# Cross-attention experts and a quantised mixture of experts in one kernel: a new order of the first blocks

## The reference

```python
def xattn(h, token_ids, W):                 # W = ctx_2048, [4, 512, 512], used three times
    expert_ids = minimum(clip(token_ids, 0, 24999) // 6250, 3)
    for e in range(4):
        g = silu(h @ W[e].T);  u = h @ W[e].T
        y = (g * u) @ W[e].T                # ctx used as the down matrix too
        out = where(expert_ids == e, y, out)

def ffn(x, router_w, wg, wu, wd):           # 8 experts, ternary weights, int8 activations
    idx = argmax(x @ router_w.T)
    for e in range(8):
        g = bitlinear(x, wg[e]); u = bitlinear(x, wu[e])
        y = bitlinear(relu(g)**2 * u, wd[e])
        out += where(idx == e, y, 0)
# bitlinear: weights round(w / mean|w|) clipped to -1..1, activations round(x * 127 / max|x|)

x = x + xattn(layernorm(x), token_ids, ctx)     # x: [2048, 512] f32
x = x + ffn(layernorm(x), router_w, wg, wu, wd)
```

## Time and profile before

| | us |
|---|---|
| median of 3 runs | 268.15 (267.83 to 268.71) |
| the profiled execution | 267.64 |
| its span in the profile | 265.9 |
| PE, DVE, ACT, POOL busy | 236.1, 214.0, 212.8, 159.6 |

### The profile page before, as it was taken

The page is one execution under the profiler, slowest core; times in us unless marked ns, Lnnn a source line. Parts: engine busy times, 40 slices in busy tenths (PEclk is TensorE's granted clock), DMA queues, the critical chain, the costliest instruction groups (busy, mean ns, idle before and its releaser), DMA issues.

```text
span 265.9 us, 5805 instructions
## 1 busy us (share of the span) xinstructions
PE 236.1 (89%) x1413; PEld 173.5 (65%) x1423; DVE 214.0 (81%) x678; ACT 212.8 (80%) x324; POOL 159.6 (60%) x315
## 2 busy tenths in 40 slices
PE   2285868999999999999999999989969999999980
PEld 2133747888888888888888888877435555555530
DVE  5947898888887787878887887778869899989971
ACT  1886777698898788898888798886779999999960
POOL 4435014477778777767776766257826477556553
PEclk9997999999999999999999999999999999999996
DMA  5997339466654555684556653353257798311110
GB/s 210 429 409 284 137 158 355 159 235 212 220 202 126 198 210 222 255 296 153 211 208 223 210 207 108 160 161 106 110 182 259 251 301 290 119 41 65 60 41 0
DMA packets 13839, 51.72 MB, mean 195 GB/s; under 512 B 2862, under 2 KB 2862, under 8 KB 10224
## 3 DMA queue, kind: packets, MB, share of 16 engines
q1 hardware_dynamic: 8928, 37.91, 39.3%
q0 software_dynamic: 4880, 13.44, 14.3%
HBM read 40.49 MB, written 13.48 MB: 203 GB/s over the span
## 4 chain that ended last, share of the span: by engine, by line
PE 72%; DVE 10%; issue 6%; POOL 5%; DMA 4%; ACT 1%; SPq 0%; POOLq 0%; DVEq 0%
PE bank L1296 35%; PE bank L1397 17%; PE bank L1289 9%; PE bank L1369 5%; PE bank L1391 3%; DVE ctx_lo L828 2%; DMA x<-x_rows,gather 2%; DMA x_rows<-row,store_at 1%; POOL out_rows L529 1%; DMA late_rows<-x_rows 1%; POOL x L434 1%; DVE ternary L796 1%; DVE ternary L851 1%; PE bank L1315 1%; DVE stats L884 1%
## 5 line engine op out<-in xcount | busy, mean ns | idle before, releaser
L1397 PE MATMUL bank<-ternary,qT 128*128 x179 | 43.4, 379 | 0.4
L566 ACT ACTIVATE ternary<-staged 128x2048 bf16<-128x2048 f32 x22 | 42.0, 1910 | 1.2 <-DMA staged<-weight_chunks 1.2
L572 ACT ACTIVATE ternary<-staged,w_scale 128x1536 int16<-128x1536 f32 x22 | 34.5, 1566 | 3.3 <-DVE w_scale L840 3.3
L485 POOL DMA_INDIRECT x_rows<-row,store_at x19 | 25.0, 1314 | 15.6 <-DVE var_eps L892 8.5
L1397 PEld LDWEIGHTS bank<-ternary,qT 128*128 128x128 bf16 x184 | 17.7, 97 | 20.7 <-issue 4.6
L529 POOL DMA_INDIRECT out_rows<-late_rows x18 | 19.8, 1102 | 16.0 <-DVE late_rows L1140 14.3
L434 POOL DMA_INDIRECT x<-x_rows,gather x19 | 21.2, 1114 | 11.5 <-DVE row L934 6.0
L444 POOL TENSOR_TENSOR rstd<-var_eps,half_powers 128x1 f32<-128x1 f32 x19 | 12.5, 657 | 20.7 <-DVE var_eps L892 20.2
L600 ACT ACTIVATE pT_hi<-bank 128x512 fp32r<-128x512 f32 x19 | 11.3, 596 | 15.7 <-PE bank L1289 15.6
L1397 PE MATMUL bank<-ternary,rT 128*128 x87 | 22.6, 379 | 1.0 <-ACT rT L664 0.8
L1296 PE MATMUL bank<-ctx_hi,hT_hi 128*128 x76 | 22.5, 417 | 0.0
(11 more groups left out here) (213 smaller groups left out, 655.8 us busy)
## 6 DMA issues: line engine op xcount, KB each, us to landing
staged<-weight_chunks SPq DMA_DIRECT2D x22, 1024.0 KB, 5.5
late_rows<-x_rows SPq DMA_DIRECT2D x18, 260.0 KB, 3.3
ternary<-ctx_chunks SPq DMA_DIRECT2D x4, 1024.0 KB, 10.9
x_rows<-filler SPq DMA_DIRECT2D x9, 260.0 KB, 5.8
ternary<-weight_chunks SPq DMA_DIRECT2D x2, 1024.0 KB, 5.5
staged<-x_rows SPq DMA_DIRECT2D x5, 260.0 KB, 2.8
x<-x_rows,gather POOLq DMA_INDIRECT x19, 3.5
x_rows<-row,store_at POOLq DMA_INDIRECT x19, 3.4
```

What stands on the lines that cost most here:

```text
L485: pool.indirect_dma_start(x1_rows, bass.IndirectOffsetOnAxis(ap=store_at[b % ROWS][:, :], axis=0), row[b % ROWS][:, :], None, bounds_check ...
L566: nc.scalar.activation(ternary[:, m * K * D:(m + 1) * K * D], staged[i % 2][:, :], ACT.Abs, accum_out=abs_sum[:, 2 * i:2 * i + 1]).then_in ...
L572: nc.scalar.activation(ternary[:, m * K * D + DVE_COLS:(m + 1) * K * D].bitcast(I16), staged[i % 2][:, DVE_COLS:], ACT.Copy, scale=w_scale ...
L1397: last = pe.matmul(ps[:, :], left[:, k * P:(k + 1) * P], ternary[:, bass.ds(e * (3 * K * D) + (kind * K + k) * D, D)], start=(k == 0), sto ...
```

## The change

- **Sorting.** `place_block` is stored as an integer, which rounds it, so the instruction with `MAGIC` (L787) goes. The product of `block_hot` with `token1` goes from DVE to GpSimd, between its first and second tile; GpSimd has three tiles and DVE thirteen. PE takes GpSimd's tiles together before its last. `gather1` is made by one instruction (with 0 instead of -1 where there is no token) before the experts' table.
- **Loads.** SP waits for the fence behind the second gather, and then issues weights 2, context 2, weights 3, context 3. Weights 2 and 3 go into places of their own (matrices 8 to 11 of `ternary`), and weights 4 and 5 take the buffers of 0 and 1.
- **GpSimd** issues four gathers in its prologue with the first power between the third and fourth, and then makes the high halves of the contexts 2 and 3, which ACT did.
- **Layernorm.** h is only x minus its mean; the factor rstd is applied in silu's scale and in the gate (`scalar_tensor_tensor` instead of `tensor_tensor`). So `normalise` waits for the mean alone, and silu waits for rstd. GpSimd's `inverse_deviation(b)` waits for the gate of block b - 2 instead of its h.
- **DVE.** Low halves are made in two instructions of 1024 columns, set between the statistics; those of context 3 stand at the end of tick 2. `variance` is split into `aggregate` and `variance`. The cuts of the matrices 0 to 3 go to the end of the ticks 5 to 8. In tick 2 mean and scale of matrix 4 stand behind `largest`.
- **PE.** `first_product(0)` waits in three steps; products 1 to 3 wait for the low half of their own block's expert, product 4 for all. `WARM_UP` is 4, 5, 4. `sum_mean(0)` stands before the first block's expert is read; `transpose_h(2)` before `sum_mean(3)`; in tick 2 `sum_mean(4)` behind `first_product(2)`.
- **ACT.** In tick 2 `scale_part(4)` stands behind `evict_hT(3)`.

```diff
-WARM_UP = (4, 8, 4)
+WARM_UP = (4, 5, 4)
...
-        place_block = sb("place_block", [P, TILES], F32)
+        place_block = sb("place_block", [P, TILES], I32)
...
+        staged_early = [spare(8, 2 * K * D, F32), spare(10, 2 * K * D, F32)]
+        def staged_of(i):
+            return staged_early[i - 2] if i in (2, 3) else staged[i % 2][:, :]
...
-        POOL_TILES = TILES * 2 // 7
+        POOL_TILES = 3
...
             def load_weights(i):
-                if i >= 2:
-                    sp.wait_ge(dve_part, i - 1)
-                    sp.wait_ge(act_part, i - 1)
-                sp.dma_start(staged[i % 2][:, :], weights_in[ORDER[i]]).then_inc(staged_in[i % 2], 16)
+                if i in (2, 3):
+                    sp.dma_start(staged_of(i), weights_in[ORDER[i]]).then_inc(staged_early_in[i - 2], 16)
+                    return
+                if i >= 4:
+                    last = i - 4 if i < 6 else i - 2
+                    sp.wait_ge(dve_part, last + 1)
+                    sp.wait_ge(act_part, last + 1)
+                sp.dma_start(staged_of(i), weights_in[ORDER[i]]).then_inc(staged_in[i % 2], 16)
             load_context(0)
             load_weights(0)
             load_context(1)
             load_weights(1)
+            sp.wait_ge(gathering, 2)
+            load_weights(2)
             load_context(2)
+            load_weights(3)
             load_context(3)
...
-            for i in range(2, len(ORDER)):
+            for i in range(4, len(ORDER)):
                 load_weights(i)
...
             for t in range(POOL_TILES):
                 pool.tensor_scalar(row_hot[:, t, :], iota16[:, :], place_row[:, t:t + 1], None, ALU.is_equal)\
                     .then_inc(pool_hot_ready, 1)
+                if t == 0:
+                    pool.wait_ge(flagged, 1)
+                    pool.tensor_tensor(block_hot, block_hot, token1[:, :, None].to_broadcast(wide), ALU.mult)\
+                        .then_inc(blocks_hot_ready, 1)
...
+            def high_halves(e):
+                pool.wait_ge(ctx_in_sem[e], 16)
+                pool.tensor_copy(ctx_hi[:, e * K * D:(e + 1) * K * D], ctx_raw[e]).then_inc(pool_hi_ready, 1)
...
                 if b >= 2:
-                    pool.wait_ge(h_ready, b - 1)
+                    pool.wait_ge(p_ready, b - 1)
                 pool.wait_ge(var_ready, b + 1)
...
             gather(0)
-            pool.memset(fence[:, :], 0.0).then_inc(gathering, 1)
+            pool.memset(fence[:, :1], 0.0).then_inc(gathering, 1)
             gather(1)
+            pool.memset(fence[:, 1:2], 0.0).then_inc(gathering, 1)
+            gather(2)
             inverse_deviation(0)
-            gather(2)
+            gather(3)
             inverse_deviation(1)
-            gather(3)
+            high_halves(2)
+            high_halves(3)
...
+                if i in (2, 3):
+                    act.wait_ge(staged_early_in[i - 2], 16)
+                else:
+                    act.wait_ge(staged_in[i % 2], 16 * (i // 2 + (i < 2)))
+                nc.scalar.activation(ternary[:, m * K * D:(m + 1) * K * D], staged_of(i), ACT.Abs,
...
+                act.wait_ge(rstd1_ready, b + 1)
                 if b >= 1:
                     act.wait_ge(pT_ready, b)
-                nc.scalar.activation(p[:, :], a_ps[b % 2][:, :], ACT.Silu).then_inc(sil_ready, 1)
+                nc.scalar.activation(p[:, :], a_ps[b % 2][:, :], ACT.Silu, scale=rstd1[b % 2][:, :])\
+                    .then_inc(sil_ready, 1)
...
-            high_halves(2)
+            evict_hT(0)
             scale_part(1)
-            evict_hT(0)
-            high_halves(3)
...
-                scale_part(t + ABOVE)
+                if t > 2:
+                    scale_part(t + ABOVE)
...
+                if t == 2:
+                    scale_part(t + ABOVE)
...
             link(dve.tensor_scalar(place_block[:, :], place[:, :], 1.0 / P, 0.5 / P - 0.5, ALU.mult, ALU.add))
-            link(dve.tensor_scalar(place_block[:, :], place_block[:, :], MAGIC, MAGIC, ALU.add, ALU.subtract))
             dve.scalar_tensor_tensor(place_row[:, :], place_block[:, :], -float(P), place[:, :], ALU.mult, ALU.add)\
                 .then_inc(placing, 1)
             wide = [P, TILES, B1]
-            link(dve.tensor_tensor(block_hot, iota[:, None, 0:B1].to_broadcast(wide),
-                                   place_block[:, :, None].to_broadcast(wide), ALU.is_equal))
-            dve.tensor_tensor(block_hot, block_hot, token1[:, :, None].to_broadcast(wide), ALU.mult)
+            dve.tensor_tensor(block_hot, iota[:, None, 0:B1].to_broadcast(wide),
+                              place_block[:, :, None].to_broadcast(wide), ALU.is_equal).then_inc(flagged, 1)
...
+            table_ps = bank[6][:, 0:B1]
+            dve.wait_ge(sort_pe, 2)
+            dve.tensor_scalar(gather1[:, :], table_ps, -1.0, 0.0, ALU.add, ALU.max).then_inc(sorted1, 1)
...
-            def low_halves(e):
-                cols = slice(e * K * D, (e + 1) * K * D)
-                dve.wait_ge(ctx_hi_ready, e + 1)
-                dve.tensor_tensor(ctx_lo[:, cols], ctx_raw[e], ctx_hi[:, cols].bitcast(F32),
-                                  ALU.subtract).then_inc(ctx_lo_ready, 1)
+            def low_half(e, part):
+                first = part * K * D // 2
+                cols = slice(e * K * D + first, e * K * D + first + K * D // 2)
+                if part == 0:
+                    dve.wait_ge(*((ctx_hi_ready, e + 1) if e < 2 else (pool_hi_ready, e - 1)))
+                ins = dve.tensor_tensor(ctx_lo[:, cols], ctx_raw[e][:, first:first + K * D // 2],
+                                        ctx_hi[:, cols].bitcast(F32), ALU.subtract)
+                if part == 1:
+                    ins.then_inc(ctx_lo_ready, 1)
...
-                dve.wait_ge(rstd1_ready, b + 1)
+                dve.wait_ge(moments_ready, b + 1)
                 if b >= 1:
                     dve.wait_ge(hT_ready, b)
-                dve.tensor_scalar(h[:, :], x[b % RING][:, :], moments[b % 2][:, 0:1], rstd1[b % 2][:, :],
-                                  ALU.subtract, ALU.mult).then_inc(h_ready, 1)
+                dve.tensor_scalar(h[:, :], x[b % RING][:, :], moments[b % 2][:, 0:1], None, ALU.subtract)\
+                    .then_inc(h_ready, 1)
...
-                dve.tensor_tensor(p[:, :], a_ps[b % 2][:, :], p[:, :], ALU.mult).then_inc(p_ready, 1)
+                dve.scalar_tensor_tensor(p[:, :], a_ps[b % 2][:, :], rstd1[b % 2][:, :], p[:, :],
+                                         ALU.mult, ALU.mult).then_inc(p_ready, 1)
...
-            low_halves(0)
-            scale_part(0)
+            low_half(0, 0)
             moments_of(0)
+            aggregate(0)
+            normalise(0)
             variance(0)
             mean_of(1)
             scale_of(1)
-            normalise(0)
+            low_half(0, 1)
...
                 if t == 2:
-                    cut(3)
+                    low_half(3, 0)
+                    low_half(3, 1)
+                if 5 <= t < 9:
+                    cut(t - 5)
...
+            pe.wait_ge(blocks_hot_ready, 1)
             for i in range(TILES - POOL_TILES):
+                if i == TILES - POOL_TILES - 1:
+                    for t in range(POOL_TILES):
+                        pe.wait_ge(pool_hot_ready, t + 1)
+                        pe.matmul(bank[6][:, 0:B1], row_hot[:, t, :], block_hot[:, t, :], start=False, stop=False)
...
-            def product1(ps, hi, lo, e):
+            def product1(ps, hi, lo, e, first=False):
                 pairs = [(hi, ctx_hi), (hi, ctx_lo), (lo, ctx_hi)]
                 for n, (left, right) in enumerate(pairs):
+                    if first and n == 1:
+                        pe.wait_ge(ctx_lo_ready, 1)
+                    if first and n == 2:
+                        pe.wait_ge(hT_lo_ready, 1)
...
+                if b == 0:
+                    pe.wait_ge(hT_hi_ready, 1)
+                    pe.wait_ge(ctx_hi_ready, 1)
+                    pe.wait_ge(centred, 1)
+                else:
+                    pe.wait_ge(hT_lo_ready, b + 1)
                 if b >= 2:
                     pe.wait_ge(p_ready, b - 1)
-                if b == 0:
-                    pe.wait_ge(centred, 1)
-                if b < E1:
-                    pe.wait_ge(ctx_lo_ready, b + 1)
-                product1(a_ps[b % 2], hT_hi, hT_lo, expert_of[b]).then_inc(a_ready, 1)
+                if 1 <= b < E1:
+                    pe.wait_ge(ctx_lo_ready, expert_of[b] + 1)
+                if b == E1:
+                    pe.wait_ge(ctx_lo_ready, E1)
+                product1(a_ps[b % 2], hT_hi, hT_lo, expert_of[b], b == 0).then_inc(a_ready, 1)
...
+            sum_mean(0)
             pe.wait_ge(experts1_ready, 1)
             load_expert(0)
-            sum_mean(0)
...
+            transpose_h(2)
             sum_mean(3)
-            transpose_h(2)
...
-                sum_mean(t + ABOVE)
+                if t > 2:
```

(3 more changed lines are left out.)

68 lines of the change are left out of this document (35 added, 33 removed).

## The result

| | before | after |
|---|---|---|
| median of 4 runs each, us | 267.99 (267.50 to 268.71) | 272.06 (271.92 to 273.09) |
| ratio to before | | 1.0158 (95% interval 1.0124 to 1.0193) |
| span of the profiled execution | 265.9 | 270.1 |

What follows compares the result with a forecast made beforehand. PE was taken as the bound from 51.7 us on; the start gives 4.7 us, the fill takes 0.6 back, moving tick 4 from 56.58 to 52.5: -4.0 us from the median 268.15 gives 264.2, range 262.0 to 267.4.

Steps and rivals of the forecast that it cites:

- To the first product: Start of the kernel: gathers go out and land sooner, so the first product starts at 20.7 us instead of 25.36.
- Rival 3: First gather: its own start-up, not the queue, takes the 7.1 us; tick 4 gains only 0.3 us, 267.9; chance 0.05.
- 2.5 us apart: Loads behind the second fence: third matrix lands at 20.8 us, then context 2, fourth matrix, context 3 at 2.5 us spacing.
- 0.7 us for nothing: Third matrix in the fill: ACT is busy until 21.5 us, so it may land 0.7 us late without cost.
- PE idle 1.1: Block 1's first product waits for the second half of ctx_lo 1 until 26.6 us, PE idle 1.1 us.
- GpSimd's copies: High halves of contexts 2 and 3 on GpSimd: 3.2 us each; up to 6 us each cost nothing.
- rival 2: GpSimd's copies run at the one-hot's rate, 11.2 us each, putting tick 4 at 61.9; 273.5 us, chance 0.08.
- Rival 1: Early blocks: GpSimd and DVE, or loads and gather 2, hold each other up; tick 4 gains 2.0, 266.2; chance 0.19.
- All behind it moves along, if PE stays the bound: From tick 4's start on PE: later ticks of 7.98 us and the second phase shift with it, by -4.0 us.
- Loss in the ticks: Further loss in the ticks, shown by idle PE in ticks 5 to 8: near 268.5 us, chance 0.05.
- Edits at nothing: Three-operand gate (0.68 against 0.69 us) and silu's scale cost nothing; cuts 0.6 us each in ticks 5 to 8, covered.

Runs made afterwards that it cites:

- unhook: Changed kernel with DVE's hT_lo(4) ahead of block 5's statistics and PE's sum of matrix 6 behind tick 4's first product; 271.00 us, ratio 1.0129.
- low3early: Changed kernel with DVE's two low-half instructions for context 3 put back ahead of tick 2; 266.98 us, ratio 0.9921.
- final: w6first plus warm1's eight matmuls, two in the passage, castwait's wait with scale part 1 behind h(2), and unhook's earlier hT_lo(4); 264.68 us, ratio 0.9839.
- nofence: w6first without SP's wait for the fence behind the second gather; 271.37 us, ratio 1.0116.
- warm1: w6first plus eight matmuls whose results nothing reads, in PE's idle time ahead of block 1's first product; 265.50 us, ratio 0.9907.
- w6first: Changed kernel with two loads exchanged: SP issues weights 6 before the extra matrix; 266.75 us, ratio 0.9923.
- clock: Changed kernel plus unread matmuls in PE's idle time: nine in tick 4, two in the passage; 269.95 us, ratio 1.0051.
- unfold: w6first with rstd put back into h and taken out of silu and the gate; 268.67 us, ratio 0.997.
- silu0: w6first with block 0's silu and gate and block 1's first product moved ahead of work on matrix 2; 268.26 us, ratio 1.0004.
- acthigh: w6first with the high halves of contexts 2 and 3 moved back from GpSimd to ACT; 268.72 us, ratio 0.9995.
- castwait: warm1 with GpSimd's copy of context 2 waiting until DVE has made ctx_lo 1; 267.20 us, ratio 0.9944.
- both: w6first with silu0's order, six unread matmuls ahead of block 1's first product and two in the passage; 268.11 us, ratio 1.0018.

## Why the prediction was wrong

- **To the first product: right.** GpSimd's product took 0.69 us (forecast 1.1, bounds 0.56 and 1.7), the gather landed in 4.03 us (3.5), and the first product started at 20.16 (20.7) and was 2.9 us long (2.8). The list was ready at 12.2 (11.5), because `place_row` ended at 8.52 instead of 7.86; in unhook, low3early and final it ended at 7.8, so these 0.7 us differ between executions. Rival 3 falls, and nofence shows that the fence did it.
- **The loads behind the fence: mis-sized.** "2.5 us apart" took no account of the gathers and the filler beside them. The third matrix landed at 23.0 (20.8), contexts 2 and 3 at 27.3 and 32.3 (23.3, 28.3). The third matrix was given 0.7 us for nothing and came 2.2 late, and ACT's queue had silu(0) behind it: gate(0) at 25.61 instead of 24.2, first_product(1) at 28.23 instead of 26.6. In other executions they came sooner: in unhook, with the same prologue, the third matrix before 21.6, context 2 at 24.2 and first_product(1) at 27.32. But that product ran at the low clock for longer, so that tick 3 started no sooner (45.91, 45.84 in the changed kernel). What the late loads cost at tick 4 is not separated.
- **"PE idle 1.1" had a price that the sum left out.** The forecast named that wait and went on with 2.85 us for the product; it took 4.52, at a clock of 0.5. The same prediction had read a half clock behind idle PE in the earlier trace rows. Of the 2.1 us that tick 4 was late (54.61 for 52.5), some 1.5 are this: to the transposes behind it the product took 4.3 us, in warm1 2.8. The pair with equal loads is unhook, unedited up to tick 3, and warm1 (context 2 at 24.2 and 24.5): 5.3 and 2.8 us for the product, tick 3 at 45.91 and 44.22, tick 4 at 54.66 and 52.93.
- **GpSimd's copies: within the bounds** (1.9 us alone, forecast 3.2, bounds 1.8 and 11.2; rival 2 falls). **Rival 1 is a real mechanism**: copies and these DVE instructions exclude each other, 0.8 us on a scale part here (1.26 for 0.48), 0.95 to 1.3 us on the low half ahead of first_product(1) in warm1 and w6first. It was given less than half for the one-hots of the earlier trace rows, which run side by side; that row was no test of a copy.
- **The step that failed:** "All behind it moves along, if PE stays the bound". The prediction followed the low halves of context 3 on DVE to 42.9 to 45.1 us, but not who waits for them: SP, for the extra matrix, with weights 6 behind it. It looked at the new wait on SP and not at the old one whose condition had been moved. The 5.2 us of tick 4 are this, by w6first and low3early; some 1.6 of them are the half clock behind the wait (clock). Loss in the ticks had a chance of 0.05, and its sign was to be idle PE in ticks 5 to 8, not in tick 4. The range was said to leave out rival 2 and half of the last; it left out rival 3 (267.9) too.
- **Edits at nothing.** The gate takes 0.75 and not 0.69 us, silu 0.68 and not 0.59; both off the path in the ticks. The cuts in ticks 5 to 8 cost nothing: PE is gapless from 60 to 172 us. The fold pays at the first block, where unfold's h(0) waits 0.70 us for the power, and more at block 2, where h waits 3.13.

## What to carry to other kernels

Where a step moves later, list every engine that waits for it, SP's queue first: a load that waits there holds all loads behind it, and they go out together, in front of the next gather. Price an idle moment of PE as its length plus, where the clock may fall, the slower product behind it, and fill it with matmuls nobody reads where it can't be removed. When an instruction moves back on one engine, move back what waits for it on the others, or work that needs nothing of it waits too (silu0). One profile is one execution: the same prologue met loads 3 us apart and two levels of the clock. Before work goes to GpSimd, look which DVE instructions run at that time.

## What the runs showed of the hardware

- **A gather is held up by the megabytes queued around it.** It landed in 3.6 us with one load queued 2 us ahead (w6first), in 7.96 with two ahead and a third issued 1.9 us behind it, and in 8.0 behind the queue of eight (nofence). The Trainium skill (DMA: Bandwidth & Descriptors, Queues, rings and completion order) says that a DMA engine takes turns between its queues packet by packet. By that, as an estimate for equal packets, a gather of 0.26 MB would have been held for little more than its own length. Here it landed 2.4 us behind the second of the two loads, and most of the third load moved in that time: from 52.0 to 57.5 us the DMA engines were 99% busy, at 404 GB/s. The gather does not wait for everything queued, either: that of 16.06 us landed at 24.0, ahead of contexts 2 and 3 (27.3 and 32.3), which were issued 0.2 and 1.2 us behind it. The measurement decides, and why it is so stays open.
- **Idle PE does not always lose the clock.** w6first and the changed kernel are the same up to tick 3, with the same short waits of PE near 41 us (0.83 and 0.72 us, and 0.80 and 0.73). From 37.9 to 45.0 us the changed kernel (first row) kept its clock and w6first (second) lost it:

```profile
37.90:45.00 7.10, 5.58 (x29) 4.29 (x28) 5.16 (x15) 7.00 (x11) 4.03 (x9) 1.00 0.14 38
```

```profile
37.90:45.00 7.10, 5.55 (x26) 4.15 (x25) 5.12 (x16) 7.00 (x10) 3.82 (x8) 0.88 0.14 38
```

The wait of 0.96 us in the passage lost it in the profiles of the changed kernel, unhook, warm1 and acthigh, not in those of the kernel before, w6first, low3early, silu0, nofence, castwait and unfold. With two matmuls in it (clock, both, final; 0.51 us of idle time left) it was kept each time. The times go with it: beside the runs warm1 to nofence the kernel before took 266.6 to 267.0 us at a mean clock of 0.990 to 0.992, and 270.3 at 0.973. What decides it in one execution was not tried.
